# Moving one dense half ahead of the weighing, and the coordinates between the halves, on TensorE and VectorE

## What is computed

```python
# layer 0: attention with 4 heads of 32 channels over all 4096 points, around a residual
xn = group_norm(x, norm_w, norm_b)
q, k, v = split(einsum('bchw,oc->bohw', xn, qkv_w) + qkv_b)
attn = softmax(einsum('bhqd,bhkd->bhqk', q, k) * hd ** -0.5)
x = einsum('bchw,oc->bohw', attn @ v, proj_w) + proj_b + skip
# layer 1: deformable convolution, 3 x 3 taps, 8 groups of 16 channels
offset_feat = conv1x1(concat([x, feat_s * 2]), W_off)
om = conv3x3(offset_feat, W_om) + b_om           # offsets y, offsets x, mask
out = relu(deform_conv_v2(feat_s, offset, sigmoid(mask), W_dcn, b_dcn)) + x
```

## Time and profile before

| | |
|---|---|
| time, median of 3 runs | 14781.15 us (14759.02 to 14793.24) |
| profiled execution, its time | 14777.67 us |
| profiled execution, its span | 14775.8 us |
| PE busy | 10555.4 us, 71% |
| PE weight loads busy | 6336.2 us, 43% |
| DVE busy | 8145.2 us, 55% |
| ACT busy | 5947.3 us, 40% |
| POOL busy | 8738.5 us, 59% |
| mean granted clock of PE | 0.882 |

### The profile page before, as it was taken

The page is one execution under the profiler, slowest core; times in us unless marked ns, Lnnn a source line. Parts: engine busy times, 40 slices in busy tenths (PEclk is TensorE's granted clock), DMA queues, the critical chain, the costliest instruction groups (busy, mean ns, idle before and its releaser), DMA issues. The chain is left out here.

```text
span 14775.8 us, 188241 instructions
## 1 busy us (share of the span) xinstructions
PE 10555.4 (71%) x64244; PEld 6336.2 (43%) x64244; DVE 8145.2 (55%) x11571; ACT 5947.3 (40%) x7640; POOL 8738.5 (59%) x18437
## 2 busy tenths in 40 slices
PE   5666677776777777777577777777757777777775
PEld 1244344443444444444344444444434444444455
DVE  4355455555555555554555555556455565555554
ACT  1334344443344444444244444444424444444443
POOL 0354566665566556666376666567736675665688
PEclk7888899997899998999788998889979899989988
DMA  1211100000010000000001000000100100000000
GB/s 51 67 50 50 52 21 19 17 17 21 16 25 17 18 18 19 18 18 18 16 19 24 18 17 18 17 18 18 24 12 18 25 19 18 19 16 18 17 19 21
DMA packets 341082, 341.02 MB, mean 23 GB/s; under 512 B 113056, under 2 KB 203552, under 8 KB 340000
## 3 DMA queue, kind: packets, MB, share of 16 engines
q0 software_dynamic: 196608, 201.72, 6.6%
q10 hardware_dynamic: 97920, 71.35, 1.5%
q1 hardware_dynamic: 45472, 54.53, 1.4%
HBM read 283.11 MB, written 44.04 MB: 22 GB/s over the span
## 5 line engine op out<-in xcount | busy, mean ns | idle before, releaser
L474 POOL DMA_INDIRECT g<-patches,idx x6144 | 6120.3, 996 | 992.6 <-issue 891.3
L712 PE MATMUL ps_x<-fx,hats 128*128 128x208 f32 x18432 | 3786.7, 357 | 930.4 <-DVE dval L1070 872.8
L907 DVE TENSOR_REDUCE mx<-ring 128x2 f32<-128x1024 f32 x2048 | 2412.4, 1221 | 3352.4 <-PE ring L670 3338.6
L712 PEld LDWEIGHTS ps_x<-fx,hats 128*128 128x128 f32 x18432 | 3283.3, 196 | 1660.1 <-issue 1400.8
L546 ACT ACTIVATE p<-ring 128x1024 f32<-128x1024 f32 x2048 | 1978.0, 1017 | 2981.9 <-PE ring L728 2821.7
L445 POOL TENSOR_TENSOR carrier<-carrier 128x1 f32<-128x1 f32 x512 | 111.9, 218 | 4929.3 <-DVE idx L1014 3002.0
L725 PE MATMUL ring<-qf,kf 32*128 32x512 f32 x8192 | 1494.5, 804 | 2062.7 <-ACT hats L556 1365.5
L470 POOL TENSOR_TENSOR carrier<-carrier 128x1 f32<-128x1 f32 x11776 | 2533.8, 243 | 102.5
L1069 DVE TENSOR_TENSOR ps_x<-ps_x,chosen 128x416 f32<-128x416 f32 x1536 | 919.6, 599 | 2387.0 <-PE ps_x L712 2373.2
L565 ACT ACTIVATE hats<-hats,ones_s 128x1024 f32<-128x1024 f32 x1536 | 1679.6, 1140 | 25.0
L738 PE MATMUL ps_a<-p,v 128*64 128x512 f32 x4096 | 1420.6, 780 | 2.1 <-ACT p L546 2.1
(11 more groups left out here) (125 smaller groups left out, 7655.1 us busy)
## 6 DMA issues: line engine op xcount, KB each, us to landing
g<-patches,idx POOLq DMA_INDIRECT x6144
patch_in<-in_fpad ACTq DMA_DIRECT2D x544, 64.0 KB
patches<-patch_out ACTq DMA_DIRECT2D x136, 256.0 KB
fx<-in_fpad SPq DMA_DIRECT2D x20, 416.0 KB, 7.8
p<-in_x SPq DMA_DIRECT2D x4, 2048.0 KB, 9.6
xq<-in_x SPq DMA_DIRECT2D x32, 256.0 KB, 2.8
fs_s<-in_fs SPq DMA_DIRECT2D x32, 256.0 KB, 2.7
xs<-in_x SPq DMA_DIRECT2D x32, 256.0 KB, 2.6
```

Source lines behind the costliest of these rows:

```text
L474: nc.gpsimd.indirect_dma_start(out=g[:, j, :], out_offset=None, in_=patches[b], in_offset=bass.IndirectOffsetOnAxis(ap=idx[:, t, j:j + 1], ...
L712: last = mm(cells, hats[:, i % HATS, 1 + pair, j * 128:(j + 1) * 128], fx[:, pair, :, group * GC:(group + 1) * GC], start=pair == 0, stop= ...
L907: V.tensor_reduce(mx[:, n:n + 2, c], ring[slot][:, :, :], AX.X, ALU.max).then_inc(ring_free[slot], 1)
```

## The change

It moves calls within the kts of PE's and DVE's `step`; no instruction is added or removed. On PE the first (or only) half of a kt now stands between the scores and the weighing; the coordinates of kts above 0 stand right behind the first chunk of maxima, ahead of the second half; kt 0 keeps its coordinates where they were. Where a kt has two halves, the first is half 1 of the set begun in the kt before, and the second is half 0 of the next set. On DVE the first half of a kt stands ahead of the new features and of the maxima, the second where both stood. The order of the ring is the same. ACT, GpSimd and SyncE are unchanged.

```diff
--- before.py
+++ after.py
@@ -799,12 +799,15 @@
                     scores(s, uses, 0)
                     scores(s, uses, 1)
                 for kt in key_tiles(s):
-                    maxima = maxima_at(s, last, kt)
+                    maxima, halves = maxima_at(s, last, kt), halves_at(s, kt)
                     if attends(s):
                         if 1 <= kt < KT - 1:
                             scores(s, uses, kt + 1)
                         if not last and kt == KT - 1:
                             max_to_rows(s + 1, uses, "rows")
+                    for r, t, i, half in halves[:1]:
+                        blocks_of_half(b, r, t, i, half, second)
+                    if attends(s):
                         weigh(s, uses, kt)
                     if maxima and kt == MAX_KT[0]:
                         pe.wait_ge(q_ready, s + 2)
@@ -812,7 +815,10 @@
                         scores_for_max(uses, ("max", m), m)
                     if kt == 0 and projects(s - 1):
                         project(s - 1, uses)
-                    for r, t, i, half in halves_at(s, kt):
+                    if kt > 0:
+                        for r, t, i in hats_at(s, kt):
+                            distances(uses, r, t, i)
+                    for r, t, i, half in halves[1:]:
                         blocks_of_half(b, r, t, i, half, second)
                     for r, t in aligned_at(s, kt):
                         align(tile_number(r, t))
@@ -820,8 +826,9 @@
                         turn_part(r, t, part)
                     if kt == 0 and projects(s - 1):
                         offset_features(s - 1, uses)
-                    for r, t, i in hats_at(s, kt):
-                        distances(uses, r, t, i)
+                    if kt == 0:
+                        for r, t, i in hats_at(s, kt):
+                            distances(uses, r, t, i)
                     if kt == 1 and attends(s) and not last:
                         queries(s + 1, uses, "queries")
                     if convolves(s - 1) and 2 <= kt < 2 + conv_uses(s - 1):
@@ -1092,11 +1099,14 @@
                         if not last:
                             rows_of_max(uses, "rows")
                         project(s)
+                    halves = halves_at(s, kt)
+                    for r, t, j, half in halves[:1]:
+                        dense_half(r, t, j, half)
                     if kt == 0 and projects(s - 1):
                         new_features(s - 1, uses)
                     for m in maxima_at(s, last, kt)[:1]:
                         maxima(uses, ("max", m), m)
-                    for r, t, j, half in halves_at(s, kt):
+                    for r, t, j, half in halves[1:]:
                         dense_half(r, t, j, half)
                     for r, t, j in weighed_at(s, kt):
                         weigh_hats(r, t, j)
```

## The result

The changed kernel takes 14935.17 us (median of 3 runs, 14934.82 to 14938.51) against 14781.15: slower by 1.07% (ratio 1.0107, 95% interval 1.0084 to 1.0130), 154 us where 304 were forecast. The profiled execution has a span of 14936.4 us (14775.8) and a mean granted clock of 0.855 (0.882).

A forecast was written before the change was run, and what follows sets the result against it. A loop of waits, with no engine full, was taken to bound the kernel. Waits (-3.9) and clock (+16.2) gave +12.3 per step, +344 over 28 steps, less 40 for last steps: 15,085 us from 14,781.15; range 14,600 to 15,340.

The forecast's parts named there:

- The moved waits, kt by kt: Each kind of kt rebuilt at full clock with the new orders; moved waits alone give -3.9 us of a 430 us step.
- The coordinates' wait for the maxima: PE's coordinates (L694) newly wait for VectorE's first maxima reduction, about 1.2 us, some 600 times.
- The clock decides: PE's low clock behind 16 changed pauses of a step adds +16.2 us; +12.3 per step with the waits.
- the single long pause that I had priced at 1.4: At 5 two-half kts with transposes and coordinates per step, one pause of 3.1 us, costing 1.4 through low clock.
- The 0.8 for pauses before the change: Low-clock price taken for each of PE's pauses in the kernel before: 0.8 us, from 0.55 to 1.6.
- Two of the signs that I had named: Signs of a right forecast: kt 13 near 9 us, and scores at 2.09 in over half of the kts.
- Twenty-eight equal steps: The +12.3 us per step was taken for all 28 steps with maxima: +344 us.
- Not slower (rival): PE's clock stays as it is, pauses get no dearer than 0.8 us: 14,610 us; chance 0.22.
- Much slower: Rival: every one of the 16 changed pauses of a step costs 2.45 us: 15,370 us; chance 0.12.
- The transposes' rule: Full clock doesn't engage for transposes between PE's new pauses, so 11 pauses cost 2.45 us each, sum 15,225 us.

The follow-up runs named there:

- the run with fewer fillers: Changed kernel plus 5 and 10 matmuls that compute nothing (9 and 19 in an earlier run) in each one-half kt with maxima and coordinates: 14633.47 us.
- The run with the coordinates alone: Kernel before with only the coordinates moved, right behind the first chunk of maxima, both halves left in place: 15512.65 us, ratio 1.0472.
- the run where ACT reads first: Changed kernel, with ACT reading the coordinates ahead of copying the turned samples: 14197.47 us, ratio 0.9588 to the kernel before.
- the half alone: Changed kernel with the coordinates back behind the transposes, so only the first half moves ahead of the weighing: 14553.68 us, ratio 0.9827.

## Why the prediction was right, and by how much it wasn't

- **The moved waits, kt by kt:** the pieces were right. At the full clock the maxima matmuls start 5.46 behind the scores (forecast 5.55), kt 11 takes 11.23 (11.25), kt 10 13.91 and kt 22 13.83 (14.2), and in the run with fewer fillers kt 12 11.80 (12.0 to 12.25), kt 13 8.85 (8.85), kts 17 and 25 10.54 (2.35 less than before; in the steps before that ran them at the full clock they took 12.9 to 13.3).
- **The coordinates' wait for the maxima:** forecast about 1.2, some 600 times; 559 times, 747.5 us, 1.34 each. The run with the coordinates alone shows that their move is the harm, the run where ACT reads first that ACT's order is worth 738 us of the changed kernel's time.
- **The clock decides:** that low clock costs time of its own is shown by fillers that made the changed kernel faster by 302 us. Its size per pause came out uneven: 1.6 at kt 12 and kt 23 (12.86 against 11.23 for the same kind of kt at the full clock), 2.2 at kt 13, nothing at kts 11 and 19. These two and kt 23 all follow the single long pause that I had priced at 1.4. The 0.8 for pauses before the change is not shown as a mean. An ordinary step became 12.1 longer against 12.3 forecast; with terms that came out this uneven, and 13.7 in the steps that took 430 before, so close a sum is in part luck. Two of the signs that I had named failed: kt 13 took 11.04 and not near 9, as the low stretch reached into it, and a third of the scores, not over half, take the full 2.09.
- **Twenty-eight equal steps: this is the term that failed.** The prediction multiplied one step by 28. The first steps, in which ACT also makes the tables, aren't like it: the wait for the exponentials, 0.82 in the earlier trace rows, was over 2 there and all but went, and the three intervals came out 102 us shorter where +37 was put down. That 139 is nearly all of the gap between 304 and 154. That it is the early half that wins there, the two separate moves show: with the half alone these three are 150 us shorter, with the coordinates alone 90 longer. One late step couldn't show it; the waits taken over the first 1800 us would have.
- **Not slower (rival):** it wanted the clock's price unchanged; the clock over 1200 us fell from 0.91 to 0.88. It didn't come. **Much slower** neither: it wanted 22.5 more per step, and 12.1 came.
- **The transposes' rule:** the upper price by it, 2.45, wasn't reached, and the run with transposes as fillers gives the clock of matmul fillers, 0.899. Where the Trainium skill (TensorE: Matmul & The Clock Gate, Part 4: PE-mode transpose) says that the full clock doesn't engage for transposes, these runs differ for the fp32 transposes of this kernel, and the measurement decides.

## What to carry to other kernels

A move that takes away a visible wait is paid by what used to lie in the shadow of the moved work: here the coordinates' slot was free only because a half had stood before them, and moving one half in one-half kts took that cover away for nothing. Ask of each reader in the chain what stands ahead of it in its own order; in kt 10 PE's coordinates came 7.6 us behind the scores instead of 10.4, and ACT read them at 11.3 instead of 11.4, until ACT's two calls changed places. And take a step from every phase of the kernel before multiplying: the first steps had another engine late.

## What the runs showed of the hardware that was not expected

- Work that computes nothing can make a kernel faster: 15 filler calls in each one-half kt with maxima and coordinates brought 14935 to 14633 us, since at the low level (1.2 GHz) scores take 2.09 instead of 1.14 and a half up to 4.5 instead of 2.4 us.
- The low stretches don't stand behind every pause. In the changed kernel kt 11 ran at 1.00 and kt 12 at 0.79 though PE had paused over 2.5 us ahead of both; mending some pauses moved them to others (fillers in the kernel before: kt 17 from 0.87 to 1.00, kt 22 from 1.00 to 0.89).
- Transposes held the granted clock at 0.899 exactly as matmuls did, with half the filling time (2.0 us against 3.8 a kt).
